# One core, attention and FP4 feed-forward block: the transposed halves of normalised x are made in SBUF and turned by DMA instead of on TensorE

## The reference

```
xn  = (x - mean) / sqrt(var + 1e-5)
qkv = xn @ W_qkv.T                     # 16 heads of 16
q   = softmax(q) / 4 ; k = exp(k)
    # causal linear attention in buckets of 64 tokens: a bucket reads the sums
    # of k*v and of k over all buckets before its own
attn = q @ context / max(q @ sum_k, 1e-6)
x + attn @ W_out.T
  + fp4(silu(fp4(xn) @ fp4(w_gate).T) * (fp4(xn) @ fp4(w_up).T)) @ fp4(w_down).T
```

## Time and profile before

| | |
|---|---|
| time, median of 3 runs | 1378.86 us (1377.84 to 1379.21) |
| the profiled execution | 1378.78 us, its span 1377.1 us |
| busy: TensorE matmuls | 1301.7 us, 95% of the span |
| busy: VectorE | 1294.4 us, 94% |
| busy: ScalarE | 1028.2 us, 75% |
| busy: GpSimd | 250.1 us, 18% |
| mean busy share of the 16 DMA engines | 39.6% in SyncE's queue |
| instructions | 41687 |

### The profile page before, as it was taken

One profiled execution on the slowest core, in us unless ns is written; L12 is line 12 of the kernel. 1 busy time (PEld: TensorE's weight loads), 2 busy tenths in 40 slices (PEclk: granted clock), 3 DMA queues, 4 the chain that ended last, 5 costly groups with the idle time before them and its releaser, 6 DMA issues.

```text
span 1377.1 us, 41687 instructions
## 1 busy us (share of the span) xinstructions
PE 1301.7 (95%) x10318; PEld 913.1 (66%) x10318; DVE 1294.4 (94%) x3901; ACT 1028.2 (75%) x3349; POOL 250.1 (18%) x664
## 2 busy tenths in 40 slices
PE   0279999999999999999999999999999999999996
PEld 0257676677767677676767677676766767676674
DVE  6769999999999999999999999999999999999996
ACT  1577778777787878777787877778787777878772
POOL 2211212111121211112121111112111111212110
PEclk9889999999999999999999999999999999999998
DMA  4023444444344444334444433434444343434334
GB/s 124 4 38 64 91 89 84 88 93 87 78 102 87 84 89 95 83 80 95 92 85 88 97 83 81 99 85 84 88 98 89 76 96 85 92 81 99 81 69 89
DMA packets 362747, 116.85 MB, mean 85 GB/s; under 512 B 327772, under 2 KB 362204, under 8 KB 362716
## 3 DMA queue, kind: packets, MB, share of 16 engines
q1 hardware_dynamic: 361990, 115.80, 39.6%
q10 hardware_dynamic: 726, 0.72, 0.2%
HBM read 19.99 MB, written 16.78 MB: 27 GB/s over the span
## 4 chain that ended last, share of the span: by engine, by line
PE 92%; DVE 4%; ACT 1%; issue 1%; DMA 1%; SPq 0%; DVEq 0%; ACTq 0%
PE outp L1168 11%; PE nump L1118 6%; PE unit1a L1058 6%; PE unit0a L1058 6%; PE outp L1170 5%; PE unit1a L1060 5%; PE unit1a L1062 5%; PE unit0a L1060 5%; PE unit0a L1062 5%; PE ctxp L1128 4%; PE unit1b L1058 4%; PE unit1b L1060 4%; PE unit1b L1062 4%; PE unit0b L1058 4%; PE unit0b L1060 4%; PE unit0b L1062 4%
## 5 line engine op out<-in xcount | busy, mean ns | idle before, releaser
L1168 PE MATMUL outp<-w_down_cat,q_rows 128*128 128x256 f16 x1408 | 246.0, 274 | 0.0
L599 ACT ACTIVATE snap<-ctxp,mask 64x68 f32<-64x68 f32 x1024 | 236.1, 308 | 3.2
L409 POOL TENSOR_TENSOR var_scaled<-squares,var_mul 128x1 f32<-128x1 f32 x128 | 33.5, 262 | 947.8 <-ACT scratch L492 947.8
L1168 PEld LDWEIGHTS outp<-w_down_cat,q_rows 128*128 128x128 f16 x1408 | 138.3, 98 | 16.5
L1170 PE MATMUL outp<-w_down_lo,q_rows 128*128 128x256 f16 x640 | 147.6, 274 | 0.0
L517 ACT ACTIVATE xnt<-trp 128x256 f16<-128x256 f32 x256 | 97.3, 380 | 58.5 <-PE trp L1082 58.5
L562 ACT ACTIVATE th<-unit1a,c_g 128x352 f32<-128x352 f32 x128 | 70.9, 554 | 83.8 <-PE unit1b L1062 83.8
L562 ACT ACTIVATE th<-unit0a,c_g 128x352 f32<-128x352 f32 x128 | 71.0, 555 | 83.0 <-PE unit0b L1062 81.8
L810 DVE TENSOR_REDUCE blk<-h 128x44 f32<-128x704 f32 x128 | 123.8, 967 | 0.1
L863 DVE TENSOR_TENSOR hx_v<-h,blk 128x704 f32<-128x704 f32 x128 | 112.1, 876 | 0.0
L400 POOL TENSOR_TENSOR att_s<-att,att_s 128x256 f16<-128x256 f32 x128 | 86.5, 676 | 124.2 <-ACT att_s L554 124.2
(11 more groups left out here) (203 smaller groups left out, 4156.4 us busy)
## 6 DMA issues: line engine op xcount, KB each, us to landing
xring<-x SPq DMA_DIRECT2D x128, 128.0 KB, 2.7
out<-xring SPq DMA_DIRECT2D x128, 128.0 KB, 2.5
xqt<-xq_s SPq DMA_TRANSPOSE x128, 2.4
att_t<-att_s SPq DMA_TRANSPOSE x128, 2.5
q_rows<-q_rows SPq DMA_TRANSPOSE x128, 3.6
raw_qkv<-wqkv_t SPq DMA_DIRECT2D x1, 768.0 KB, 4.3
raw_up<-wup ACTq DMA_DIRECT2D x2, 352.0 KB
raw_gate<-wgate SPq DMA_DIRECT2D x2, 352.0 KB
```

Of the source, the lines that this page charges most:

```text
L599: nc.scalar.activation(kept[:, :, cols], sums[:, :, cols], ACT.Copy, scale=mask[rows, f, h:h + 1])\
L1168: nc.tensor.matmul(downp, hqt[:, par, m, :], w_down_cat[:, m, :], start=(m == 0), stop=False)
```

## The change

The high half of normalised x is now made by ScalarE from `xn` in SBUF (`high_xn`, after the mean and ahead of the copy of q), the low half by GpSimd (`low_xn`, behind `low_att` and ahead of the rstd chain). Both go to a new tensor `xn_s`, in which the tokens stand on the partitions. SyncE turns it with a fourth transposing DMA a tile into `xnt` (`turn_xn`, for tile k+3, behind h's). `project_qkv` waits for that DMA. TensorE's two transposes, its subtraction and ScalarE's two copies out of PSUM for x are gone, and with them `minus16`. The transposes of q now wait only for the copy of the q before, since no one else uses the bank `trp`.

```diff
@@ buffers
-        minus16 = sb("minus16", [P, P], fp16)
+        xn_s = sb("xn_s", [P, 2, 2, D], fp16)
@@ SyncE
+            def turn_xn(t, par):
+                if not is_tile(t):
+                    return
+                sp.wait_ge(xn_lo, after(t))
+                sp.sem_inc(sp_turn, 1)
+                if begun(t - 2):
+                    sp.wait_ge(qkv_done, after(t - 2))
+                sp.sem_inc(sp_turn, 1)
+                sp.dma_start_transpose(xnt[:, par, :, :].rearrange("p s (c k) -> p (s c) k", k=P),
+                                       xn_s[:, par, :, :].rearrange("p s k -> p (s k)")).then_inc(xn_turned[par], 16)
+
             def turn(i):
                 for d in range(2):
                     turn_xq(2 * i + d + 1, 1 - d)
                     turn_att(2 * i + d - 1, 1 - d)
                     turn_h(2 * i + d - 1, 1 - d)
+                    turn_xn(2 * i + d + 3, 1 - d)
...
+            turn_xn(0, 0)
             turn(-1)
@@ GpSimd
-            nc.gpsimd.tensor_tensor(minus16[:, :], zeros16[:, 0:P], ident16[:, :], ALU.subtract).then_inc(minus_ready, 1)
+            def low_xn(t, par):
+                if not is_tile(t):
+                    return
+                pool.wait_ge(xn_hi, after(t))
+                nc.gpsimd.tensor_tensor(xn_s[:, par, 1, :], xn[:, par, :], xn_s[:, par, 0, :], ALU.subtract).then_inc(xn_lo, 1)
...
                 low_att(k - 1, odd)
+                low_xn(k + 3, odd)
                 rstd_of(k + 4, par)
@@ ScalarE
                 if begun(t - 2):
-                    act.wait_ge(xnt_tr, after(t - 2))
+                    act.wait_ge(xn_lo, after(t - 2))
...
-            def split_xnt(t, par, part):
-                if not is_tile(t):
-                    return
-                act.wait_ge((xnt_tr, xnt_less)[part], after(t))
-                if part == 0 and begun(t - 2):
-                    act.wait_ge(qkv_done, after(t - 2))
-                nc.scalar.activation(xnt[:, par, part, :], tr32, ACT.Copy).then_inc(xnt_split, 1)
+            def high_xn(t, par):
+                if not is_tile(t):
+                    return
+                act.wait_ge(xn_done, after(t))
+                if begun(t - 2):
+                    act.wait_ge(xn_turned[par], turned(t - 2, par))
+                nc.scalar.activation(xn_s[:, par, 0, :], xn[:, par, :], ACT.Copy).then_inc(xn_hi, 1)
...
                 tanh_gate(k, 0, par)
-                split_xnt(k + 2, par, 0)
                 normalise_waits(k + 3)
                 mean_waits(n, d + 4)
-                split_xnt(k + 2, par, 1)
                 tanh_gate(k, 1, par)
                 factor_of_row(k - 1, odd)
                 normalise(n, d + 3)
                 mean_of(n, d + 4)
+                high_xn(k + 3, odd)
@@ TensorE
-            def transpose_xn(t, par):
...
-            def less_xn(t, par):
...
             def project_qkv(t, par):
                 if not is_tile(t):
                     return
-                pe.wait_ge(xnt_split, after(t, 2))
+                pe.wait_ge(xn_turned[par], turned(t, par))
...
                 pe.wait_ge(q_exp, after(t))
-                pe.wait_ge(xnt_split, after(t + 1, 2))
+                if begun(t - 1):
+                    pe.wait_ge(qt_done, after(t - 1))
...
                 gate_up(k, 0, par)
-                transpose_xn(k + 2, par)
-                gate_up(k, 1, par, (0,))
-                less_xn(k + 2, par)
-                gate_up(k, 1, par, (1,))
+                gate_up(k, 1, par)
                 transpose_q(k + 1, odd)
```

More of the change, by code:

```diff
@@ L177, in linear_attention_fp4_ffn_block @@
         consts = sem("consts")
-        minus_ready = sem("minus_ready")
         w_max = sem("w_max")
@@ L191, in linear_attention_fp4_ffn_block @@
         xn_done = sem("xn_done")
-        xnt_tr = sem("xnt_tr")
-        xnt_split = sem("xnt_split")
-        xnt_less = sem("xnt_less")
+        xn_hi = sem("xn_hi")
+        xn_lo = sem("xn_lo")
+        xn_turned = [sem(f"xn_turned{par}") for par in range(2)]
         qkv_done = sem("qkv_done")
@@ L1049, in _ @@
             pe.wait_ge(consts, 7)
-            pe.wait_ge(minus_ready, 1)
             def clear_context():
```

## The result

The changed kernel takes 1360.49 us (median of 4 runs, 1359.18 to 1362.24), the kernel before 1379.03 in the same comparison. The ratio is 0.9866, 95% interval 0.9849 to 0.9883: faster by 18.5 us, where the forecast's sum had 38.4. The profiled execution took 1361.72 us, its span is 1360.0.

What follows compares the result with a forecast made beforehand. TensorE bound the kernel at 10.03 us a step, VectorE close behind. VectorE's floor of 9.69 plus 0.03 for the snapshots gave 9.72; 124 x 0.31 = 38.4 us saved, so 1340 us, range 1330 to 1362.

Steps and rivals of the forecast that it cites:

- a longer VectorE floor: VectorE's step if only its listed idle of 0.24 us went: 9.79 us, giving 1349 us.
- the snapshot chain: Rival: ScalarE's snapshots, then TensorE's context matmuls, set the step at 9.84 us; 1355 us, chance 0.15.
- TensorE's relief: Two transposes and the subtracting matmul gone from TensorE: 0.39 us a step, leaving 9.64 us alone.
- VectorE's floor: VectorE's instructions unchanged, only 0.34 us of waiting goes: 9.69 us a step, making VectorE the bound by 0.05 us.
- The chain through the snapshots: Second tanh, snapshots, context matmuls, projections: 9.56 to 9.76 us with ScalarE's new copy; 0.03 us a step charged.
- SyncE's queue: One more DMA transpose a tile, taking 1.47 us of queue with 1.47 us to spare in the tighter step: cost 0.
- GpSimd's own time: One more subtraction of 0.68 us on GpSimd, busy 18.7% of the stretch: costs nothing.
- The first steps: In the first two steps proper TensorE waits for the snapshots, a chain losing 0.39 and gaining as much: no gain.
- What GpSimd does to VectorE: New GpSimd subtraction against VectorE instructions with two SBUF operands: bounds 0 to 0.35 us a step, taken as 0 to 0.01.
- the drift: A VectorE losing time to the new GpSimd subtraction shifts to where it loses none; the gap before line 916 fits it.
- The port in part: Rival: new subtraction lands on lines 916 and 918, holding VectorE 0.25 us a step; 9.94 us, 1368 us, chance 0.11.
- The rival on the slower side: Subtraction just ahead of line 905 or 916 every step, VectorE stands 0.68 us: 10.37 us, 1421 us, chance 0.06.

Runs made afterwards that it cites:

- the first experiment: The changed kernel plus one GpSimd wait: the attention's subtraction starts only after VectorE's two scale instructions of the same step; 1334.49 us, ratio 0.9679 against the kernel before.
- the relief and the wait: Kernel before without TensorE's transposes and subtraction for x and ScalarE's two copies, nothing replacing them, plus GpSimd's wait for the two scale instructions; 1332.15 us, ratio 0.9656.
- The relief experiment: Kernel before, with TensorE's transposes and subtraction for x and ScalarE's two copies left out and nothing in their place; 1353.61 us, ratio 0.9814.
- the kernel with the early wait: The changed kernel with the attention's subtraction on GpSimd waiting only for h's block maximum, one VectorE instruction too early; 1446.54 us, ratio 1.0497.
- the kernel with two copies: The changed kernel with GpSimd's wait for the two scale instructions, and ScalarE's new copy done twice; 1351.93 us, ratio 0.9814.

## Why the prediction was wrong

The direction, the order of the bounds and most terms held. The time, 1360.5 us, even lies in the range of 1330 to 1362, but that is luck: the upper end was drawn for a longer VectorE floor or for the snapshot chain, neither of which came, and the gain of 18.5 us is less than half of the 38.4 forecast.

- **TensorE's relief.** It is at least 10.03 - 9.68 = 0.35 us a step: with the meetings out of the way TensorE is busy 999.32 of 1000 us at a step of 9.68, and VectorE is full too. The whole 0.39, and that TensorE alone would need 9.64, no run shows. In the changed kernel TensorE waits for VectorE, so the order of the two was right.
- **VectorE's floor, 9.69 us.** Right: 9.68 in the first experiment.
- **The chain through the snapshots.** It had more slack than I gave it, about 9.5 us against 9.56 to 9.76, and didn't bind. From the last snapshot to the context matmuls it is 0.46 us in the mean with the relief and the wait, where the copy is missing, and 0.30 in the first experiment: the copy took 0.16 of it and not 0.32 to 0.42. The 0.03 us a step that I charged for it isn't there: the kernel with the wait is at 1334.5, where my sum, with nothing for the port, had 1340.
- **SyncE's queue, GpSimd's own time.** Cost nothing that was seen. The first steps, which I had at no gain, gave some 2 us.
- **What GpSimd does to VectorE: this step failed.** This is contention between GpSimd and VectorE, the "port" of the prediction. I took 0 to 0.01 us a step, and it is 0.23: 124 x 0.23 = 28.5 us, and 26.0 us in the measured times (1360.5 against 1334.5), more than the whole miss of 20. Three errors were in it. I looked only where the new subtraction would land, and left the old one, line 400, where it was in the trace of before. I counted only VectorE instructions with two SBUF operands, though the small tensor_scalar instructions of one operand are held too. And I took the drift for a cure ("A VectorE that loses time here drifts to where it loses none"). The relief experiment shows the reverse: with the relief, the rest runs earlier against VectorE, and the old subtraction, which mostly stood just behind lines 826 and 830, moves onto line 826 and stays on it, in half of the steps, over the whole stretch. In the kernel with the early wait x's subtraction meets line 923 in all 94 steps; ScalarE's path to it starts from a wait for VectorE, so it moves along with VectorE. That a meeting moves the next one stands to reason from the steps that take turns, but wasn't isolated.
- **The rivals.** The port in part had the mechanism and 0.11 of the chance, but the wrong instructions (916 and 918), and 1368 us. The rival on the slower side did happen, in the kernel with the early wait: x's subtraction ahead of the second half of h's scaling in every step, at 0.44 us and not 0.68: the instruction began 0.09 us behind the subtraction and needed only 0.38 us more once that had ended, of its usual 0.52. (The chances as given add up to 0.90 for faster and 0.06 for slower, where 0.89 and 0.07 are written.)

The Trainium skill, "SBUF — State Buffer", section "Who interferes with whom", also names tensor_scalar among the instructions that can, when their operands allow it, run in a mode which takes the shared ports. The trace agrees: 0.64 us for line 843 beside GpSimd's subtraction, 0.17 without. I had used that section's sentence on two inputs only.

## What to carry to other kernels

When the bound moves from one engine to another, all that was timed against the old bound moves against the new one. Before a relief is priced, move every GpSimd instruction, the untouched ones first, against VectorE, and look at what of VectorE it then covers. Try more than the relief itself: here 0.39 us of it went with a shift of 0.94. Where a meeting costs and GpSimd has time to spare, a wait that starts its instruction behind the VectorE instructions it would hold can cost nothing: here one line made 1360.5 us into 1334.5. Set one VectorE instruction too early, the same line made it 1446.5.

## What the runs showed of the hardware

- GpSimd's subtraction of 0.67 us holds a VectorE tensor_scalar of 16 or 44 float32 elements a partition until it ends: up to 0.64 us in place of 0.17, and 0.62 to 0.76 in place of 0.25. Halved in width (0.43 us), the subtraction stretches line 849 to 0.52.
- A VectorE tensor_tensor with two operands in SBUF is held too (0.96 us in place of 0.52, line 922). Where it starts first, by 0.02 us at 332.48, GpSimd's subtraction is the one that takes longer: 1.02 us in place of 0.67.
- Reductions, reciprocals and instructions with an operand in PSUM are not held in any of these runs, nor is a tensor_scalar of one element a partition: line 872 takes 0.10 us at 600.88 in the kernel with two copies, under a subtraction from 600.56 to 601.23. In the first experiment the subtraction of 709.73 lies over line 860, a reciprocal of 60 elements, whose mean is what it was before (line 842):

```profile
L860 DVE RECIPROCAL blk<-blk 128x60 f32<-128x60 f32 x103 | 53.3, 518 | 0.0
```

```profile
L842 DVE RECIPROCAL blk<-blk 128x60 f32<-128x60 f32 x100 | 51.8, 518 | 0.0
```

- VectorE's instruction can be stamped as started 0.04 us before GpSimd's and still stand for all of it (700.93 and 700.97 in the kernel with the early wait).
